# Index limit on the gathers of the second pass of a sparse graph-attention layer

## What is computed

```python
h = relu(layernorm(x))
U = softmax(where(adj > 0, leaky_relu(h @ a1 + (h @ a2).T), -9e15), axis=1)   # 8192 x 8192, sparse
prop_u = U @ h                                    # first pass
rowsum = sum(U * 0.5 * U, axis=1)
feat = shrink(h and prop_u - h * rowsum, 1e-6)    # mixed by sigmoid(temp)
pu = U @ feat                                     # second pass
out = x + mix(feat, pu, rowsum, h0)
```

## Time and profile before

| | us |
|---|---|
| time, median of 3 runs | 1517.84 (1516.83 to 1520.83) |
| span of the profiled execution | 1535.4 |
| POOL busy over the span | 589.9 (38%), 649 instructions |
| DVE busy | 931.9 (61%) |
| PE busy | 968.4 (63%) |
| gathers in the page's groups, second pass, L634 and `W` tiles | 140, 956 ns each |

### The profile page before, as it was taken

The page is one execution under the profiler, slowest core; times in us unless marked ns, Lnnn a source line. Parts: engine busy times, 40 slices in busy tenths (PEclk is TensorE's granted clock), DMA queues, the critical chain, the costliest instruction groups (busy, mean ns, idle before and its releaser), DMA issues.

```text
span 1535.4 us, 27679 instructions
## 1 busy us (share of the span) xinstructions
PE 968.4 (63%) x3566; PEld 578.1 (38%) x3630; DVE 931.9 (61%) x5233; ACT 863.7 (56%) x1840; POOL 589.9 (38%) x649
## 2 busy tenths in 40 slices
PE   3545767776676767667777777753464564555656
PEld 3421345443333344334343333332343343333333
DVE  7756656667778788888888888875211122223333
ACT  4663777777788888888888888831221111111111
POOL 1004344443332233322222222245656565556553
PEclk9975687889899898897878788865677676767777
DMA  7989878889899999999999999822545455556665
GB/s 190 357 292 353 322 291 300 326 327 346 330 360 369 377 368 371 361 378 394 371 385 374 372 374 376 327 62 65 150 122 145 127 161 163 158 168 180 184 184 164
DMA packets 152837, 423.14 MB, mean 276 GB/s; under 512 B 31111, under 2 KB 114697, under 8 KB 136406
## 3 DMA queue, kind: packets, MB, share of 16 engines
q1 hardware_dynamic: 122492, 345.66, 61.0%
q0 software_dynamic: 30304, 77.05, 16.7%
HBM read 398.37 MB, written 33.90 MB: 282 GB/s over the span
## 4 chain that ended last, share of the span: by engine, by line
DVE 31%; issue 26%; PE 15%; SPq 11%; another core or an unknown queue 6%; ACT 4%; DMA 3%; DVEq 3%; ACTq 1%
PE TP L321 5%; PE ACC L693 2%; SPq L1599 2%; SPq L1609 2%; SPq L1602 2%; DVE XHO L1066 2%; PE ACC L689 2%; SPq L1601 2%; SPq L1600 2%; PE MISC L987 2%; DMA R<-in_x_dram 1%; ACT SG L309 1%; DVEq L257 1%; DVE JK L1133 1%
## 5 line engine op out<-in xcount | busy, mean ns | idle before, releaser
L309 ACT ACTIVATE SG<-W,ABOVE 128x4096 bf16<-128x4096 f32 x126 | 467.0, 3706 | 81.0 <-DVE cnt L1049 54.3
L634 POOL DMA_INDIRECT R<-haug_d,IDS x230 | 231.0, 1004 | 604.6 <-issue 591.1
L321 PE MATMUL TP<-SG,FOLD 128*128 128x512 bf16 x948 | 299.9, 458 | 4.4 <-issue 0.7
L680 ACT ACTIVATE DG<-ident,WSR 128x128 f32<-128x128 f32 x230 | 76.6, 392 | 373.5 <-remote 234.4
L1752 DVE SCALAR_TENSOR_TENSOR R<-ACC,SELF,R 128x256 f32<-128x256 f32 x63 | 30.5, 484 | 321.6 <-remote 238.3
L634 POOL DMA_INDIRECT W<-feat_d,IDR x140 | 133.9, 956 | 117.9 <-issue 117.9
L321 PEld LDWEIGHTS TP<-SG,FOLD 128*128 128x128 bf16 x1008 | 116.9, 125 | 118.8 <-issue 62.0
L689 PE MATMUL ACC<-R,DG 128*128 128x256 f32 x446 | 158.2, 502 | 2.8 <-issue 2.7
L688 PE MATMUL ACC<-XHO,ZB 128*128 128x256 bf16 x126 | 40.1, 318 | 179.6 <-ACTq L682 86.6
L689 PEld LDWEIGHTS ACC<-R,DG 128*128 128x128 f32 x446 | 100.3, 242 | 23.4 <-issue 6.8
L689 PE MATMUL ACC<-W,DG 128*128 128x256 f32 x274 | 98.9, 503 | 11.9 <-issue 11.9
(11 more groups left out here) (295 smaller groups left out, 2292.7 us busy)
## 6 DMA issues: line engine op xcount, KB each, us to landing
W<-in_adj_dram SPq DMA_DIRECT2D x128, 2048.0 KB, 13.6
haug_d<-R POOLq DMA_DIRECT2D x8, 1056.0 KB, 9.7
HTS<-haug_d SPq DMA_DIRECT2D x64, 132.0 KB
R<-in_x_dram SPq DMA_DIRECT2D x8, 1024.0 KB, 6.6
R<-in_x_dram SPq DMA_DIRECT2D x64, 128.0 KB
R<-in_L_gnn_h_dram SPq DMA_DIRECT2D x64, 128.0 KB
R<-feat_d SPq DMA_DIRECT2D x64, 128.0 KB
out_dram<-R SPq DMA_DIRECT2D x64, 128.0 KB, 1.8
```

The source lines that it names most:

```text
L309: nc.scalar.activation(SG[:, u, half(h)], W2[:, u, half(h)], ACT.Sign, scale=2.0 ** 100, bias=ABOVE[:], accum_out=DEG[:, u, h:h + 1]).then ...
L321: nc.tensor.matmul(KP[u], FOLD[:, b], SG[:, u, b * FW:(b + 1) * FW], start=False, stop=False)
L634: pool.indirect_dma_start(out=g[:, k, 0:w], out_offset=None, in_=table, in_offset=bass.IndirectOffsetOnAxis(ap=ids[:, k:k + 1], axis=0), * ...
L680: nc.scalar.mul(DG[:, u, k], ident[:], weights[:, k:k + 1])
```

## The change

Each gather of the second pass gets the index limit that the first pass has, and the two DVE operations that clipped the indices to the last row become plain copies. An idle lane's index then stays out of range, and the gather leaves that lane out instead of reading row 8191.

```diff
@@ second_gpsimd
-                    gather_slots(pool, t, RINGS[v], IDR[:, v], feat_d, F, gathered2[v])
-                gather_tail(pool, RINGS[v], IDT[:, v:v + 1], feat_d, F, gathered2[v])
+                    gather_slots(pool, t, RINGS[v], IDR[:, v], feat_d, F, gathered2[v], bounds_check=N - 1, oob_is_err=False)
+                gather_tail(pool, RINGS[v], IDT[:, v:v + 1], feat_d, F, gathered2[v], bounds_check=N - 1, oob_is_err=False)
@@ gather (tiles 1 to 3)
-                                        in_offset=bass.IndirectOffsetOnAxis(ap=IDR[:, t, k:k + 1], axis=0)).then_inc(arrived, 16)
+                                        in_offset=bass.IndirectOffsetOnAxis(ap=IDR[:, t, k:k + 1], axis=0),
+                                        bounds_check=N - 1, oob_is_err=False).then_inc(arrived, 16)
@@ stage
-                nc.vector.tensor_scalar(IDR[:, v], IDX[:, bass.ds(t, 1)].rearrange("p a k -> p (a k)"), float(N - 1), None, ALU.min)
-                nc.vector.tensor_scalar(IDT[:, v:v + 1], JT[:, bass.ds(t, 1)], float(N - 1), None, ALU.min)
+                nc.vector.tensor_copy(IDR[:, v], IDX[:, bass.ds(t, 1)].rearrange("p a k -> p (a k)"))
+                nc.vector.tensor_copy(IDT[:, v:v + 1], JT[:, bass.ds(t, 1)])
```

## The result

The changed kernel takes 1504.36 us (1503.45 to 1507.98) where the kernel before took 1519.25 (1516.83 to 1520.83): a ratio of 0.9917, 95% interval 0.989 to 0.9945. It is faster by 0.8%; 0.8% slower was forecast. The profiled execution has a span of 1502.5 us and a time of 1504.1, so span and time differ by 1.6 us. The profiled execution of before had a span of 1535.4, some 16 us more than its timed runs can have had. The two traces therefore differ by 33 us where the times differ by 15, and only what is larger than that, or what other runs repeat, is read from their difference. Of the 33 us, 11.4 lie ahead of the second pass, where the two kernels are the same.

What follows compares the result with a forecast made beforehand. The second pass was taken as bound by a chain of POOL's gather burst and a restart. Span 1535.4 + 14 (limit) - 2 (bytes) = 1547.4 us, scaled to a time of 1529.7 us, 0.8% slower; range 1506 to 1541.

Steps and rivals of the forecast that it cites:

- What bounds the kernel: Second pass, 1080 to 1536 us: no engine full; POOL's gather burst, then a restart of some 5 us, every 20.07 us.
- hold-up: Second pass: DVE and ACT stand still some 235 us in 20 waits during gather bursts, with a releaser the profile can't name.
- The limit on POOL: Second-pass gathers: the index limit adds 53 ns to each of 267, 14.2 us, taken as 14 on the path.
- That nothing gives it back: Second-pass bursts: they run without a pause, so nothing hides the limit's added time; 14 us counted in full.
- the last sentence on what would make the prediction wrong: Second pass: bursts becoming shorter or fewer, because the other engines could work during them; no size or chance given.
- Fewer bytes: Second-pass gather queue: about 27 MB in place of 35.01, the last landing sooner; 0 to 4 us gained, 2 taken.
- DVE: Second-pass staging: L1735 and L1736 become copies of 0.15 to 0.20 us; no change in time taken.
- Rival A: Second pass: the hold-up goes with bytes or the crowd on row 8191; strong form, time 1480 us; chance 0.15.
- weak form: Rival A with only the gathers' DMA time shrinking on the path: 29 us less 14, time 1503 us.
- Rival B: Second pass: the limit's time is not on the path, a longer burst eats POOL's idle time; 1518 us, chance 0.18.
- Rival C: Second-pass staging: the new copies block POOL's gathers, 22 us on top, time 1551 us; chance 0.06.
- The scale from trace to time: Whole kernel: profiled span 17.6 us above the timed median, so trace microseconds scale by 0.989; 12 us become 11.9.

## Why the prediction was wrong

*What bounds the kernel.* The two links, a burst and a restart, and that the hold-up of DVE and ACT is not a shortage of DMA: right. Half the bytes, and no bytes, left it in place. That the time would be near 1400 without the hold-up was right too: on chips without it the kernel takes 1377 us, though 53 us of the difference between the two traces of the kernel before lie in the first pass, which the forecast left out. Its ground for a hold-up "in runs without a profile too" is weaker than it looks: every timed run on record has a span and a clock of that execution beside it, so none is known to show the kernel without any recording.

*The limit on POOL.* 53 ns by 267 were forecast as 14.2 us; POOL's busy time grew by 14.2 us. Right in size and place.

*That nothing gives it back.* This step failed. I took the burst as a link of fixed content: so many gathers, with the others still until it ends, then a restart of some 5 us. The sum then adds 53 ns to every gather and leaves the rest. But the others don't stand altogether. They are slow while gathers follow each other closely, and how slow depends on how closely. At 1.30 us between gathers more of the tiles are staged while a burst still runs (53 of 64 for 42), and the pause, which the sum left as it was, is 2.9 us in the mean for 5.2. The pauses in the traces are 22 us shorter in all than those of before and 7 us shorter than those of half the bytes, so their sum is known only roughly; that the limit gains 0.8 to 0.9% where the hold-up is, with and without left-out lanes, is firm. The earlier trace rows had shown that a burst with a limit holds others up as well, and I read this as: as strongly. One burst beside another pass's work could not show that. No rival had this mechanism; only the last sentence on what would make the prediction wrong did, and of its two forms the bursts became shorter: 6.8 gathers in the mean for 9.9, in 39 bursts for 27.

*Fewer bytes.* 27 MB were forecast and 27.58 came, in 12816 packets. Their worth of 2 us agrees with what was measured: half of the bytes, 17.5 MB, gained 0.2% with the hold-up and nothing without it.

*DVE.* Copies of 181 and 149 ns were forecast as no change. Right.

*Rival A* gave 1503 us for its weak form, nearly the result, and that is luck: the limit with all bytes gains the same. The forecast's own sign for A, that the unnamed waits fall to 200 us, came true with 191; it was no sign of A, since this wait shrinks by whatever loosens the hold-up. *Rival B* has one half of the truth, that the limit's time is made good in the pauses, but not that more than it comes back. *Rival C*, the rule of the Trainium skill ("SBUF — State Buffer", on the "DVE blocks DMA" trap) that a copy in a two-port mode keeps GpSimd from writing descriptors: in the changed kernel's trace the mean of the L634 gathers is 1013 ns over a median of 1002, before 956 over 949. At 4 ns more for each of 267 that is 1 us, not 22. On a chip without the hold-up the changed kernel, with copies, took 1393.39 us where the clip with the limit took 1388.95. This difference is not the rule's: the 267 gathers have a mean of 1012 ns in both traces, and the second pass takes 359.0 us with the copies and 359.7 with the clips. The rule agrees with no trace here for copies as short as these; whether they run in a two-port mode the traces don't tell.

*The scale from trace to time.* I took the 17.6 us by which the span of before exceeds the median for a property of profiled runs. In the other profiles the span is 1.6 us below that execution's own time. So this execution was a long one, or it ran on another chip than the timed runs (on one chip the kernel before takes 1531 to 1535 us); which of the two isn't recorded. This did not change the sign.

*The size.* +12 us was forecast, -15 measured where the hold-up is, +12.8 and +15.5 where it isn't. The forecast's number fits the chips without it, and its trace was one from a chip with it.

## What to carry to other kernels

When engines take turns for a reason that the profile doesn't name, don't cost a step on one of them as if the other's share stood fixed: ask what a slower or faster step does to the engines that are held up, and test it by adding a harmless operation. If such an operation makes the kernel faster, the bound is the hold-up and not the engine alone. And compare with the kernel before on more than one chip before a change of 1% is called a gain: here the same edit was 0.8% faster on one kind and 1.0 to 1.1% slower on the other.

## What the runs showed of the hardware

The time of this kernel differed by a tenth between the chips used (1377 us on four, 1517 to 1533 on the others). Where POOL issues gathers back to back, on one kind nothing happens to the other engines, and on the other kind register and branch instructions of SP, PE, ACT and POOL itself come slowly. In the second pass of the kernel before, 135, 89, 66 and 48 of them take over 0.6 us with the hold-up and none without it. They lie in the bursts and for some 1 to 5 us after the start of a burst's last gather. DVE has one of 648: it isn't slow, it waits. A small register move of SP can then take 0.7 us, as 17 of the 60 moves of L1599 do in the kernel before (ns: shortest, median, longest), first with the hold-up and then without:

```profile
L1599 SPq MOVE R<-in_x_dram x60: 5/29/729, 1092.1 to 1522.1; - x60
```

```profile
L1599 SPq MOVE R<-in_x_dram x60: 29/29/29, 1036.7 to 1359.5; - x60
```

The hold-up needs neither bytes (0.15 MB in all: still 181 us of DVE's unnamed wait) nor an index limit, and it weakens as gathers lie further apart: pauses of 119 to 134, 98 to 112, 85 to 91 and 26 us at 1.25, 1.30, 1.33 and 1.44 us. What it is that the gathers and the other engines' instructions share, and why chips differ in it, stays open. One candidate was not tested: the recording of the execution itself. The kernel before leaves 15466 semaphore updates in the trace with the hold-up and 26784 in the one without, so the executions with slow instructions are also those that lose records, and no run on record is known to be one in which nothing was recorded.

A lane beyond the limit saves no packet: 48 packets for each gather of full rows with and without such lanes, and with all lanes beyond it 0.15 MB for 267 gathers of 128 lanes, by division about 4 bytes a lane. And the limit costs POOL some 50 ns for a gather, whether no lane is beyond it, a fifth or all: medians of 998 to 1002 ns with it, 944 to 949 without.
